# Adding the gated experts' results inside the wide heads, with no barrier between the two stages

## The reference

```python
# end of layer 2: gated experts. 4096 tokens, 8 experts, the best 2 for each token
w, sel = top_k(dist, 2); w = softmax(w)
out = 0
for e in range(8):
    h = silu(xs @ Wg[e] + bg[e]) * (xs @ W1[e] + b1[e])      # 128 -> 342
    out = out + we[:, e:e+1] * (h @ W2[e] + b2[e])           # 342 -> 128
x = x + out
# start of layer 3: 16 heads of 64, causal; queries from _layernorm(x), keys and values from a context
x = x + softmax(q @ k.T / 8) @ v @ Wo.T + bo
```

## Time and profile before

| what | value |
|---|---|
| median of 3 runs | 2082.69 us (2079.97 to 2089.26) |
| the profiled execution's own time | 2078.66 us |
| its span, first to last instruction | 2076.9 us |
| TensorE busy | 1774.7 us, 85% |
| VectorE busy | 1080.3 us, 52% |
| ScalarE busy | 912.0 us, 44% |
| GpSimd busy | 666.4 us, 32% |
| the gated experts' part in the span | 1256 to 1507.5 us |
| the wide heads' part | 1507.5 to about 1988 us |

### The profile page before, as it was taken

One profiled execution on the slowest core, in us unless ns is written; L12 is line 12 of the kernel. 1 busy time (PEld: TensorE's weight loads), 2 busy tenths in 40 slices (PEclk: granted clock), 3 DMA queues, 4 the chain that ended last, 5 costly groups with the idle time before them and its releaser, 6 DMA issues.

```text
span 2076.9 us, 48570 instructions
## 1 busy us (share of the span) xinstructions
PE 1774.7 (85%) x18884; PEld 1265.7 (61%) x18884; DVE 1080.3 (52%) x3087; ACT 912.0 (44%) x2496; POOL 666.4 (32%) x664
## 2 busy tenths in 40 slices
PE   6999985687569999988998982899279999999988
PEld 3565573566548778764555551899146666666763
DVE  5666547666441221124664553566545555555558
ACT  2333320576234444432332220667536556655625
POOL 3223201576211111112134316455512333333315
PEclk8999976888579999998998885899689999999979
DMA  5000000000000000015400001222310000000001
GB/s 170 8 13 8 2 2 20 21 11 1 6 1 1 2 2 2 1 69 220 167 9 26 12 12 39 58 57 62 87 57 7 6 1 6 6 7 1 2 1 41
DMA packets 48830, 63.59 MB, mean 31 GB/s; under 512 B 8106, under 2 KB 37701, under 8 KB 48349
## 3 DMA queue, kind: packets, MB, share of 16 engines
q1 hardware_dynamic: 44253, 51.98, 7.7%
q0 software_dynamic: 4352, 8.47, 1.3%
HBM read 32.29 MB, written 28.65 MB: 29 GB/s over the span
## 4 chain that ended last, share of the span: by engine, by line
PE 58%; issue 10%; DVE 7%; POOLq 3%; POOL 3%; DVEq 1%; DMA 1%; ACT 1%; SPq 1%; another core or an unknown queue 1%; ACTq 0%
PE single L1784 5%; PE quad L1772 5%; PE pair L569 3%; PE single L620 3%; PE single L2082 2%; PE quad L2065 2%; PE quad L2071 2%; PE quad L597 2%; PE pair L2443 2%; PE pair L1731 2%; DVE arena L767 2%; PE quad L2443 2%; PE single L2455 2%; PE quad L2420 2%; PE quad L2469 1%
## 5 line engine op out<-in xcount | busy, mean ns | idle before, releaser
L767 DVE TENSOR_REDUCE arena<-pair 128x8 f32<-128x1024 f32 x128 | 156.7, 1225 | 150.1 <-PE pair L569 146.5
L2676 POOL TENSOR_TENSOR arena<-arena 128x512 f32<-128x512 f32 x128 | 130.5, 1041 | 310.2 <-DVE arena L2599 310.2
L262 POOL TENSOR_TENSOR rstd<-var_eps,neg_half 128x4 f32<-128x4 f32 (+1 forms) x64 | 68.4, 1069 | 373.4 <-DVE var_eps L258 243.0
L745 ACT ACTIVATE arena<-quad 128x1024 f32<-128x1024 f32 x128 | 124.1, 1021 | 74.8 <-PE quad L603 74.8
L1842 ACT ACTIVATE arena<-quad,arena 128x256 f32<-128x256 f32 x256 | 110.7, 476 | 100.5 <-PE quad L1772 100.5
L569 PE MATMUL pair<-arena 32*128 32x512 f32 x512 | 152.3, 673 | 0.3 <-issue 0.3
L891 POOL TENSOR_SCALAR arena<-arena 128x512 f32<-128x512 f32 x56 | 86.9, 1567 | 201.7 <-ACT arena L689 201.7
L1925 DVE TENSOR_TENSOR arena<-single,arena 128x512 f32<-128x512 f32 x32 | 22.1, 692 | 212.9 <-PE single L1784 212.9
L2536 ACT ACTIVATE arena<-pair,arena 128x128 f32<-128x128 f32 x256 | 91.1, 381 | 90.5 <-DVE arena L2594 90.5
L1772 PE MATMUL quad<-arena,wide 128*128 128x256 f32 x512 | 121.7, 385 | 4.9 <-issue 4.1
L2536 ACT ACTIVATE arena<-quad,arena 128x128 f32<-128x128 f32 x256 | 91.1, 381 | 75.0 <-DVE arena L2594 75.0
(11 more groups left out here) (493 smaller groups left out, 4388.4 us busy)
## 6 DMA issues: line engine op xcount, KB each, us to landing
tokens_by_expert<-arena SPq DMA_DIRECT2D x22, 780.0 KB, 8.6
arena<-in_ctxT SPq DMA_DIRECT2D x32, 256.0 KB, 2.8
arena<-tokens_by_expert SPq DMA_DIRECT2D x72, 65.0 KB, 1.8
wide<-in_w SPq DMA_DIRECT2D x2, 2048.0 KB, 9.7
arena<-outputs_by_choice SPq DMA_DIRECT2D x16, 256.0 KB, 5.4
wide<-in_wgu SPq DMA_DIRECT2D x1, 2736.0 KB
x<-in_x SPq DMA_DIRECT2D x4, 512.0 KB, 7.6
out_x<-x SPq DMA_DIRECT2D x8, 256.0 KB, 2.3
```

Of the source, the lines that this page charges most:

```text
L745: act.activation(probs[n % 2][:, 8 * p:8 * p + 8, :].rearrange("p h q -> p (h q)"), T[:, 1024 * p:1024 * p + 1024], ACT.Exp).then_inc(s["s ...
L767: dve.tensor_reduce(mx[m % 2][:, 8 * p:8 * p + 8], S[:].rearrange("p (h k) -> p h k", h=8), AX.X, ALU.max).then_inc(s["s_free"], 1)
L2676: pool.tensor_tensor(part, part, inv[t % 3][:, 4 * r:4 * r + 4].unsqueeze(2).broadcast_to([P, 4, P]), ALU.mult).then_inc(s["norm_ready"], 1)
```

## The change

The two stages run in one phase, so the barrier between them is gone; each engine goes from the experts' code straight on to the heads'. The experts' stage ends after the weights `w1st` and `w2nd`, which now have a place of their own in SBUF (`choice_w`). ScalarE's scaling, GpSimd's adding, VectorE's adding and all statistics of the eight groups are taken out of it. In the heads:

- SyncE waits for the last stores and for `shifted_ready` (VectorE has finished its tiles), then loads the results of groups 0 and 1 ahead of the weights, and those of a later group g when the statistics of group g - 2 are done. Two buffers, `yg`, hold one group each.
- VectorE adds each group by itself: `add_results` is eight instructions x = y * weight + x on 128 x 128, four for each choice with a drain behind each four, and `stats_of`. Group 0 is added first of all, group 1 between the k pieces and `maximum(0)`, group g = 2 to 7 in slot 8 (g - 2) + 2, behind the copy of the early k piece.
- GpSimd's `rstd_results` follows: for group 0 first of all, for group 1 ahead of `normalise(0)`, for the others in the slot behind. `normed` waits for it.

```diff
@@ gated_experts
             def sync(sp):
...
                 for n in range(SLOTS):
                     sp.wait_ge(s[f"stored{n}"], 16 * (TILES // SLOTS))
-                for g in range(NG):
-                    for i in range(2):
-                        rows = slice((i * B + g * G) * P, (i * B + g * G + G) * P)
-                        sp.dma_start(yg[:, i, g * G:g * G + G, :], done[rows].rearrange("(r p) d -> p r d", p=P)
-                                     ).then_inc(s[f"y_in{g}"], 16)
-                barrier(sp, phase)
+                sp.wait_ge(s["shifted_ready"], 1)
...
             def scalar(act):
...
-                act.wait_ge(s["weights_ready"], 1)
-                for g in range(NG):
-                    act.wait_ge(s[f"y_in{g}"], 16 * 2)
-                    for i, w in ((0, w1st), (1, w2nd)):
-                        for j in range(G):
-                            n = g * G + j
-                            mm = act.activation(yg[:, i, n, :], yg[:, i, n, :], ACT.Copy, scale=w[:, n:n + 1])
-                    mm.then_inc(s["y_scaled"], 1)
-                barrier(act, phase)
...
             def vector(dve):
...
-                dve.drain().then_inc(s["weights_ready"], 1)
-                for g in range(NG):
-                    dve.wait_ge(s["y_added"], g + 1)
-                    dve.tensor_tensor(x[:, g * G:g * G + G, :], x[:, g * G:g * G + G, :], yg[:, 0, g * G:g * G + G, :],
-                                      ALU.add)
-                    dve.drain()
-                    stats_of(dve, g * G, bn, agg).then_inc(s["stats_ready"], 1)
-                barrier(dve, phase)
+                dve.drain()
...
             def gpsimd(pool):
...
-                for g in range(NG):
-                    both = slice(g * G, g * G + G)
-                    pool.wait_ge(s["y_scaled"], g + 1)
-                    pool.tensor_tensor(yg[:, 0, both, :], yg[:, 0, both, :], yg[:, 1, both, :], ALU.add
-                                       ).then_inc(s["y_added"], 1)
-                    if g >= 1:
-                        pool.wait_ge(s["stats_ready"], g)
-                        rstd_of(pool, (g - 1) * G)
-                pool.wait_ge(s["stats_ready"], NG)
-                rstd_of(pool, (NG - 1) * G)
-                barrier(pool, phase)
@@ wide_heads
+            def load_results(sp, g):
+                if g >= 2:
+                    sp.wait_ge(gated["stats_ready"], g - 1)
+                for i in range(2):
+                    rows = slice((i * B + g * G) * P, (i * B + g * G + G) * P)
+                    sp.dma_start(yg[g % 2][:, i, :, :], done[rows].rearrange("(r p) d -> p r d", p=P)
+                                 ).then_inc(gated[f"y_in{g}"], 16)
+
+            def add_results(dve, g):
+                dve.wait_ge(gated[f"y_in{g}"], 16 * 2)
+                for i in range(2):
+                    for j in range(G):
+                        n = g * G + j
+                        dve.scalar_tensor_tensor(out=x[:, n, :], in0=yg[g % 2][:, i, j, :],
+                                                 scalar=choice_w[:, 1 + i, n:n + 1], in1=x[:, n, :],
+                                                 op0=ALU.mult, op1=ALU.add)
+                    dve.drain()
+                stats_of(dve, g * G, bn2, agg2).then_inc(gated["stats_ready"], 1)
+
+            def rstd_results(pool, g):
+                pool.wait_ge(gated["stats_ready"], g + 1)
+                rstd_of(pool, g * G).then_inc(gated["rstd_ready"], 1)
+
             def sync(sp):
+                load_results(sp, 0)
+                load_results(sp, 1)
                 for i, name in enumerate("qkvo"):
...
                 for g in range(NG):
                     if g >= 2:
+                        load_results(sp, g)
                         ring_read(sp, ("v", g - 2, HB - 1))
...
             def vector(dve):
                 def normed(g):
+                    dve.wait_ge(gated["rstd_ready"], g + 1)
...
+                add_results(dve, 0)
                 normed(0)
...
                 for c in range(HB):
                     keep("k", 0, c)
+                add_results(dve, 1)
                 maximum(0)
...
                     for piece in early[1:2]:
                         keep(*piece)
+                    if t8 % 8 == 2 and t8 // 8 + 2 < NG:
+                        add_results(dve, t8 // 8 + 2)
                     if t8 % 8 == 4 and t8 // 8 + 2 < NG:
                         normed(t8 // 8 + 2)
...
             def gpsimd(pool):
...
+                rstd_results(pool, 0)
                 pool.wait_ge(s["cvec_ready"], 1)
                 residual(0)
+                rstd_results(pool, 1)
                 normalise(0)
                 for t8 in range(N8):
                     if t8 + 1 < N8:
                         normalise(t8 + 1)
+                    if t8 % 8 == 3 and t8 // 8 + 2 < NG:
+                        rstd_results(pool, t8 // 8 + 2)
```

More of the change, by code:

```diff
@@ L107, in program @@
         earlier = sb("earlier", [P, E * E])
+        choice_w = sb("choice_w", [P, 3, B])
         ARENA = 33 * 1024
@@ L300, in program @@
         by_tile = nc.dram_tensor("tokens_by_expert", [E * REGION + E * P, ROW], F32).ap()
+        done = nc.dram_tensor("outputs_by_choice", [2 * B * P, P], F32).ap()
+        gated_sems = {}
         routed = sem("routed")
@@ L1978, in gated_experts @@
                 "bcols_copied", "xgT_ready", "turned", "g_ready", "u_ready", "sg_ready", "hid_ready", "w_ready",
-                "y_ready", "y_copied", "ones_ready", "weights_ready", "y_scaled", "y_added", "stats_ready",
+                "y_ready", "y_copied", "ones_ready", "stats_ready", "rstd_ready",
                 *(f"tile_in{i}" for i in range(LANES)), *(f"y_in{g}" for g in range(NG)),
                 *(f"stored{i}" for i in range(SLOTS))))
+            gated_sems.update(s)
             F = 342
@@ L1986, in gated_experts @@
             tokens = arena.take([TILES, ROW])
-            yg = tokens.rearrange("p t d -> p (t d)")[:, 0:2 * B * P].rearrange("p (i b d) -> p i b d", i=2, b=B)
             xrT = [arena.take([W]) for _ in range(2)]
             half = arena.take([2 * B])
-            gap, w1st, w2nd = arena.take([B]), arena.take([B]), arena.take([B])
+            gap, w1st, w2nd = (choice_w[:, i, :] for i in range(3))
             fill, part = arena.take([E, B]), [arena.take([E]) for _ in range(3)]
@@ L2005, in gated_experts @@
             wt = [arena.take([2 * F]) for _ in range(2)]
-            bn, agg = arena.take([G, 6]), arena.take([G, 2])
             assert arena.at <= arena.held
-            done = nc.dram_tensor("outputs_by_choice", [2 * B * P, P], F32).ap()
             lg_bank, count_bank = bank[2], bank[3][:, 0:2 * UNIT * E]
@@ L2094, in tensor @@
                         second(n, pe.value_load(texp[0:1, n:n + 1], min_val=0, max_val=E - 1))
-                barrier(pe, phase)
             def scalar(act):
@@ L2314, in wide_heads @@
                 "ring_free0", "ring_free1", "ring_free2", "ring_free3"))
+            gated = gated_sems
             ring_ready = [s[f"ring_ready{b}"] for b in range(RING)]
@@ L2334, in wide_heads @@
             bo, cvec = arena.take([P]), arena.take([P])
+            yg = [arena.take([2, G, P]) for _ in range(2)]
+            bn2, agg2 = arena.take([G, 6]), arena.take([G, 2])
             vrep = probsT[1]
@@ L2700, in wide_heads, with gated_then_wide, both, run @@
             return sync, tensor, scalar, vector, gpsimd
+        def gated_then_wide(phase):
+            parts = [gated_experts(phase), wide_heads(phase)]
+            def both(i):
+                def run(eng):
+                    for part in parts:
+                        part[i](eng)
+                return run
+            return tuple(both(i) for i in range(5))
         phases = []
@@ L2707, in program @@
         makers = [lambda n: small_heads(0, n), lambda n: narrow(0, n), linear_attention, expert_choice, lambda n: small_heads(2, n),
-                  gated_experts, wide_heads, lambda n: narrow(3, n)]
+                  gated_then_wide, lambda n: narrow(3, n)]
         for n, make in enumerate(makers):
```

## The result

| | before | changed |
|---|---|---|
| median of 9 runs | 2086.57 us | 2072.21 us (2064.88 to 2079.29) |
| ratio, 95% interval | | 0.9931 (0.9910 to 0.9952) |
| profiled span | 2076.9 us | 2074.2 us |

The kernel is faster by 0.7%: 14.4 us, by the interval 10 to 19. The forecast was 17.9. One of the nine runs before took 3014.8 us, and one of those beside experiments 5 to 8 took 5302.2; the ratios and intervals leave both out. On another chip (that of experiments 5 to 8), where both kernels run some 45 us faster, the changed kernel was timed once more: 0.9909 (0.9892 to 0.9926), 18.6 us by the ratio.

What follows compares the result with a forecast made beforehand. The boundary was taken as a pure gap and the heads as bound by TensorE alone. Terms -35.6 + 2.05 + 7.2 + 8.5 = -17.9 us took 2082.7 to 2064.8 us, range 2053 to 2073.

Steps and rivals of the forecast that it cites:

- part 1: Start of the heads: without the barrier, weights land about 1481.0 us and the heads start 35.6 us earlier (33.6 to 37.1).
- Rival (e): Start of the heads: results or weights arrive late, heads start only 28 us earlier, 2072 us; chance 0.05.
- part 2: Group 1's add before the first maximum: TensorE waits for a bank at the fifth v piece, cost 2.05 us (0 to 4.1).
- part 3: Six adds inside the loop: `attend` waits 1.35 us five times and 0.5 once, cost 7.2 us (0 to 24.6).
- (b): Loop: the adds cost TensorE nothing, total -25.1 us, 2057.6 us; chance 0.08.
- (c): Heads: each of the seven adds delays TensorE by its full 4.1 us, total +1.6 us, 2084 us; chance 0.11.
- The rule on the shared port: VectorE's adds: GpSimd reading SBUF would lengthen them; priced at nothing by the rows, since GpSimd idles then.
- Rival (d): Adds: VectorE and GpSimd shut each other out, 8.3 us more per add, total +40 us, 2123 us; chance 0.04.
- part 4: GpSimd's drain at the removed barrier: owed work returns at the end of the heads, cost 8.5 us (0 to 8.5).
- rival (a): GpSimd's drain: its cost is gone for good, total -26.4 us, 2056.3 us; chance 0.27.

Runs made afterwards that it cites:

- experiment 5: The changed kernel with an extra early GpSimd drain, group 1's add moved to while the weights load, and later adds cut in three: 0.9820 of before, 2008.5 us.
- experiment 6: The changed kernel repeated without edits on the third chip, against the kernel before: 0.9909.
- experiment 7: The changed kernel with the adds of groups 2 to 7 moved right behind the reciprocal, ahead of the maximum, beside GpSimd's normalise: 1.0051 of before.
- experiment 8: The changed kernel with three more GpSimd drains, behind the last indirect DMAs to `by_tile`, behind tile 35 and behind tile 71: one run, 2019.7 us.
- experiment 3: The changed kernel with group 1's add moved behind the normalisation of group 0, while the weights load: 0.9904 of before.
- experiment 4: The changed kernel with each add of groups 2 to 7 cut into three lumps in successive slots: 0.9875 of before.
- experiment 1: The changed kernel with one more GpSimd drain in idle time, behind its last indirect DMA: 0.9873 of before.
- experiment 2: The kernel before, barrier kept, with one more GpSimd drain behind its last indirect DMA: 0.9958 of before.

## Why the forecast was right, and where it was off

**The boundary** (part 1): -34.3 us for -35.6. Right in mechanism: the weights, queued behind two groups of results, set the start. The sum is off by 1.2 because two errors partly cancel: behind the results the weights take 2.7 us more than before, where I had put in half a microsecond, and the four issues ahead of them take 1.0 us less. Rival (e), a start only 28 us earlier, falls.

**Group 1** (part 2): +6.3 us for +2.05. The wait itself is as worked out, 1.9. The term left out is the clock. It reaches its full level later: about 1 us in this execution, some 1.5 in experiments 3 to 5. And it fell twice behind the wait, the remaining 3.4 us. The falls are no part of the change: they occur in the changed kernel (twice, then once), in experiments 1, 7 and 8, and in experiment 2, whose kernel has the barrier and no add in the heads (its step from scores 2 to 3 takes 7.4 us); experiment 4 has the same wait and no fall. In the windows the three profiles without a fall (experiments 3, 4 and 5) are those whose clock reached its full level last, 7 us or more behind the biases; the six with a fall had it after 4 to 6 us, but the kernel before, after 4, has no fall either. What decides whether the clock falls there, and why the ramp is longer, stays open.

**The loop** (part 3): +7.2 forecast; 6.9 came back when the lumps were cut, 15.8 - 8.5 = 7.3 by the table. The total is right; of the single slots the profile names waits of up to 0.8 and 0.4 us, 1.2 together, for the 1.35 worked out. Rivals (b) and (c) fall: the adds are not free, and nothing carries over.

**The rule on the shared port.** The page "SBUF — State Buffer" of the Trainium skill says in "Who interferes with whom" that an instruction of VectorE with both inputs in SBUF contends with one of GpSimd that reads SBUF. Experiment 7 agrees: 3.87 us for 2.35. The row that the prediction takes for it, a copy into `mean`, has one input only and so is no case of that sentence; why it took 0.71 us no run shows. In the kernel as changed the rule costs nothing, since the two don't meet: all 64 adds take 0.34 to 0.35 us. Rival (d) had the right side but the wrong price: it has each of the eight adds held up by 1.0 us, but GpSimd does only two products there and each holds up one add, so they are longer by 1.5 us, not 8.3; the loss comes from the late maximum.

**The drain** (part 4): +8.5 forecast, 8.5 measured, and rival (a) falls. The count of DMAs in that part, 48 and 16 + 72, should be 32 and 32 + 72; the forecast took the cost from the drain's row and not from the count, so it didn't suffer. This was the term on which I had been least sure. The argument that held was that idle time had not absorbed the cost in the kernel before.

**The size.** By the table 12.2 us in one execution, 14.8 in the other (522.4 - 507.6), by the timings 14.4 and 18.6, forecast 17.9. The forecast lacks about 1.2 us at the queue, 1 to 1.5 of ramp, and 0 to 3.4 of falling clock. The forecast time, 2064.8, started from the first three runs before; with the nine, whose median is 3.9 us higher, the same sum gives 2068.7. The measured 2072.2 lies less than 1 us inside the range (2053 to 2073), and it is the time of rival (e), whose cause isn't there: the total alone would not have told the forecast from that rival.

## What to carry to other kernels

A barrier's wait can hold a cost that belongs to no stage: here 8.5 us of GpSimd drain owed by indirect DMAs. Taking away the barrier only moved it to the next one; one drain placed where GpSimd idles took it away, in the old kernel as well. Read who is last at a barrier, and ask where that goes next.

Where one engine bounds a loop, the average load of the others says little. What counts is the longest lump against the slack of one slot: 4.1 us against a slack worked out as 2.75 cost about 1.2 each time (7.3 in six), and the same work in three lumps cost nothing.

Where work is put beside another engine decides as much as which engine does it: the same adds a few instructions earlier turned 0.9909 into 1.0051.

## What the runs showed of the hardware that I had not expected

- A GpSimd drain behind indirect DMAs ends 2.7 us (32 DMAs) to 8.6 us (104) after the instruction in front of it, about 0.08 us for each DMA in four of five cases, and 0.12 in the fifth. It is paid once, and with a pow in front the drain is as long 500 us later (9.60) as after 31 us (9.61), where it is 1.1 otherwise.
- Eight VectorE instructions with both tensors in SBUF take 2.35 us alone and 3.87 beside two GpSimd products; the GpSimd ones take 2.09 instead of 2.04. The whole loss falls on two of the eight, 1.13 and 1.12 us for 0.35.
- After TensorE had waited 1.9 us in a stretch that had been busy for some 18 us, the granted clock fell to 0.50 for 3 to 4 us in some executions and not in others; it also fell so in a kernel without that wait (experiment 2).
